# Column tiles for two matmul groups, an accumulating DMA for a bias and written slot tables in a selective-scan transformer layer

## The chip, the cores and the metric

The kernel runs on one NeuronCore of a Trainium2 chip. The metric is the time of one execution in device microseconds; less is better. A profile of one execution is beside it. Everything is float32.

## The reference, cut to what matters

Input x is 4 batches of 4096 positions with 512 channels. Per batch, six modulation rows come from a small matrix product. Then:

```
h   = layernorm(x) * (1 + ca) + sa
xs, z = split(h @ w_in.T + b_in);  z = silu(z)
dt  = softplus(xs @ w_dt.T + b_dt)
B   = xs @ w_B.T + b_B;  C = xs @ w_C.T + b_C          # 16 states each
state[n] = exp(A[n] * dt) * state[n] + dt * xs * B[n]  # along the positions
y   = (sum_n state[n] * C[n] + D * xs) * z
x   = x + ga * (layernorm(y @ w_out.T + b_out + h) * gamma + beta)
h   = layernorm(x) * (1 + cb) + sb
s   = h @ Win + bin                                    # 64 features m
g_m = sum_16(relu(s_m * W1_m + b1_m) * W2_m) + b2_m
x   = x + gb * (g @ Wout + bout)
```

The last three lines and the products for B and C are what the change rewrites on TensorE.

## The kernel before, in words

The 16384 positions are cut into 32 chunks of T = 512. The program is one software pipeline of steps `s = -1 ... 33`; step s does the scan of chunk s, the front (first norm, xs, dt, B/C, first factor u) of chunk f = s+1, the gate product, output projection and second norm of chunk b = s-1 and the feed-forward of chunk c = s-2. Every full step has U = 64 **slots**, one for each (state n, channel block j) pair of the scan, i = 4n + j.

The work of a slot goes round four engines. ScalarE (ACT) makes `exp(A dt)` into a ring of 6 (line 842, `decays`, 4 slots ahead) and `v = u * B[n]` (line 852, `input_of`). TensorE (PE) turns four 128x128 blocks of v into one of the two halves of the PSUM tile `b_ps` (`turn_v`, line 530): in slot i it makes unit i+1, and first waits for scan i-1. VectorE (DVE) runs the scan over 512 positions into a ring `hs` of 6 (`scan`, line 1140), and every second slot keeps two end states (line 1148). GpSimd (POOL) multiplies two units at a time with the row C[n], spread over the partitions by a DMA into `c_bc` (`product`, line 379; ring `pr` of 10), and for four of the 16 states folds two products with an accumulating DMA (`add_products`, line 390). TensorE transposes the products into `y_ps` and sums them there (`add_unit`, line 543), four slots after the unit, or seven for folded ones.

Beside that circuit each engine does its **side work**, written as generators: a function yields the slot from which its next part may be issued, and `Beside.until(i)` issues all parts that are due in slot i, in program order. So a slot number fixes only the place in an engine's in-order queue; the waits are on semaphores. For TensorE the side work (`dense`, line 720) is the list ORDER (lines 35 to 53): `g` (feed-forward inner sum, `add_g`, line 552, 8 matmuls), `yz` (turn y), `res` (residual, line 593), `pre` (output projection, line 600, 16), `out` (feed-forward output, `add_out`, line 579, 4), `xt` and `x2` (turn the normed rows), `z` (line 692, 16), `xs` (line 629, 16), `dt` (line 658, 16), `cb` (product for C and B, `add_cb`, line 666, 4), `bt` (turn B, line 673), `ut` (turn u) and `s` (line 716, 4). Each part has a length of 1, short ones 0.5 or 0.6; `slot(part)` and `made(part)` spread them evenly over the 64 slots in proportion to those lengths. ScalarE, VectorE, GpSimd and SP (which issues the plain DMAs) take their slots from `made` of the part that they follow, plus a small written distance. So `ut.0` is issued in slot 54, `cb.0` to `cb.3` in 48, 49, 49 and 50, `out.0` to `out.3` in 9, 11, 13 and 15, `g.0` to `g.7` in 0, 0, 1, 1, 2, 3, 3 and 5.

All side results pass through two PSUM banks `dense0` and `dense1`: `long(s, group)` is the bank of the running group, `inside(s, group)` the other one for what is done meanwhile. `tmp`, `xn`, `proj` and `x1` are shared in the same way.

The operations that the change touches are these. The C/B product is `[32 outputs] x [512 positions]` for each of four channel blocks; ScalarE adds the bias into `cb_t` [32, 512] (line 970), four small transposes turn it (line 673), SP stores the C rows (line 333). The inner sum of the feed-forward packs the 16 hidden units as 8 pairs: line 874 makes `relu` for 64 features x 2 hidden units on 128 partitions, and `w2_dg[:, k, 0:64]` (two stacked diagonals, the other 64 columns zero) sums them to 64 rows of a bank. Line 890 copies that to `gm` [128, 512] with a bias that is 1 in row 64, and line 579 multiplies a 128-position block of `gm` with `wout_g`, whose row 64 is gate times `bout`: so the output bias comes with the matmul. Line 1185 adds the bank to `x1`.

Four lines say where TensorE meets the scan:

```
pe.wait_ge(S["scan_done"], at("scan_done", s, i - 1))
for tb in range(TB):
    last = turn(b_ps[:, i % 2, tb * P:(tb + 1) * P], v[:, n % V_RING, tb, j * P:(j + 1) * P])
last.then_inc(S["b_made"], 1)
```

Of the kernel before, what the change touches and what calls it, by code (L numbers as in the profile page):

```python
def build_program(nc, ap, B, L, D, N, M, INNER):
# [8 lines left out]
    P = 128  # L10
# [24 lines left out]
    ORDER = """g.0 g.1 g.2 g.3 g.4 g.5 g.6 yz.0 g.7  # L35
        res.0 yz.1 pre.0.0 yz.2 pre.0.1 yz.3 pre.0.2 out.0 pre.0.3
        res.1 pre.1.0 out.1 pre.1.1 pre.1.2 out.2 pre.1.3
        res.2 pre.2.0 out.3 pre.2.1 pre.2.2 pre.2.3
        res.3 xt.0 pre.3.0 pre.3.1 pre.3.2 pre.3.3
        z.0.0 xt.1 z.0.1 z.0.2 xt.2 z.0.3  # L40
        xs.0.0 xt.3 xs.0.1 xs.0.2 xs.0.3
        xs.1.0 xs.1.1 xs.1.2 xs.1.3
        xs.2.0 xs.2.1 xs.2.2 xs.2.3
        xs.3.0 xs.3.1 x2.0 xs.3.2 xs.3.3
        dt.0.0 dt.0.1 x2.1 dt.0.2 dt.0.3
        dt.1.0 dt.1.1 x2.2 dt.1.2 dt.1.3
        dt.2.0 dt.2.1 x2.3 dt.2.2 dt.2.3
        dt.3.0 dt.3.1 dt.3.2 dt.3.3
        cb.0 cb.1 cb.2 cb.3
        z.1.0 z.1.1 bt.0 z.1.2 z.1.3  # L50
        z.2.0 ut.0 z.2.1 z.2.2 ut.1 z.2.3
        s.0 ut.2 s.1 s.2 ut.3 s.3
        z.3.0 z.3.1 z.3.2 z.3.3""".split()
    LENGTH = dict(yz=0.6, xt=0.6, x2=0.6, ut=0.6, bt=0.5, res=0.5)
    GROUPS = ("g", "pre.0", "pre.1", "pre.2", "pre.3", "z.0", "xs.0", "xs.1", "xs.2", "xs.3", "dt.0", "dt.1", "dt.2",
              "dt.3", "cb", "z.1", "z.2", "s", "z.3")
    BEGIN, END = {}, {}
    TOTAL = 0
    for part in ORDER:
        BEGIN[part] = TOTAL  # L60
        TOTAL += LENGTH.get(part.split(".")[0], 1)
        END[part] = TOTAL
    TOTAL += 0.8

# [17 lines left out]
    def slot(*part):  # L82
        return int(BEGIN[".".join(str(n) for n in part)] * U / TOTAL)

    def made(*part):
        return int(END[".".join(str(n) for n in part)] * U / TOTAL)


    SECOND = [made("pre", tb, 3) + (5 if tb == TB - 1 else 9 - tb) for tb in range(TB)]

    ctx = ExitStack()
    with ctx:
# [6 lines left out]
        par_d = nc.dram_tensor("par_d", (3, B, D), f32).ap()  # L99
# [7 lines left out]
        w2_dg = sb("w2_dg", [P, J, P])  # L107
# [7 lines left out]
        b_cb = sb("b_cb_col", [2 * N, 1])  # L115
# [21 lines left out]
        cb_t = sb("cb_t", [2 * N, T])  # L137
# [26 lines left out]
        gamma_r, beta_r, gain_r, shift_r = (dt_t[0:B, 1, n, :] for n in range(4))  # L164
        y_ps = pb("y_ps", [P, TB, D])
# [7 lines left out]
        def inside(s, *group):  # L173
# [3 lines left out]
        N_LATE = 6 + 5 * 2 + 2  # L177
        once = """wx_loaded wd_loaded late_loaded b2_loaded const_zeroed const_masks neg_done scal_done w2top_done
        w2dg_done b_out_loaded bout_done moved_ps moved c_exp c_one c_rcp silu_c rows_ps rows_taken mods_ps mods_done sign_done gate_done par_made
        par_stored gs_loaded wg_loaded wout_done""".split()  # L180
# [3 lines left out]
            "SP": dict(stored_0=Q, stored_1=Q, stored_2=Q, stored_3=Q, c_stored=Q),  # L184
# [46 lines left out]
        def _(sp):  # L231
# [25 lines left out]
            sp.wait_ge(S["const_zeroed"], 5)  # L257
# [3 lines left out]
            load("wd_loaded", b_cb[:, :], column("b_cb"))  # L261
# [14 lines left out]
            load("late_loaded", wout_b[0:M, :], ap["Wout"])  # L276
            load("late_loaded", wout_b[M:M + 1, :], row("bout"))
            sp.wait_ge(S["const_masks"], 2)
            load("b2_loaded", b2[0:M, :], column("b2"))
# [30 lines left out]
            STORE = [made("out", tb) + 1 for tb in range(TB)]  # L310

            def step(s, has_s, has_f, has_b, has_c):
                f, b, c = s + 1, s - 1, s - 2
                for i in range(U):
# [6 lines left out]
                    for tb in range(TB):  # L321
# [4 lines left out]
                        if has_b and i == STORE[tb] + 3:  # L326
# [3 lines left out]
                    if has_f and i == made("cb", 3) + 2:  # L330
                        sp.wait_ge(S["cb_done"], at("cb_done", f, 1))
                        sp.wait_ge(S["prod_done"], at("prod_done", f - 2, U // 2))
                        sp.dma_start(c_d[f % 2], cb_t[0:N, :]).then_inc(S["c_stored"], Q)
# [15 lines left out]
        def _(gp):  # L349
            count_up(gp, "Pool")  # L350
            for t, val in ((ident[:, :], 0.0), (w_cb[:, :, :], 0.0), (w2_dg[:, :, :], 0.0), (b2[:, :], 0.0),
                           (wout_b[:, :], 0.0)):
                gp.memset(t, val).then_inc(S["const_zeroed"], 1)
            gp.wait_ge(S["const_zeroed"], 5)

            def select(view, base, pattern):
                gp.affine_select(out=view, in_=view, compare_op=ALU.not_equal, fill=1.0, base=base, pattern=pattern,
                                 channel_multiplier=1).then_inc(S["const_masks"], 1)

            select(ident[:, :], 0, [[-1, P]])  # L360
            select(b2[:, :], -M, [[0, 1]])

# [30 lines left out]
            def attended(b):  # L393
                for tb in range(TB):
                    yield made("out", tb) + 6
                    if tb == 0:
# [4 lines left out]
                    yield made("pre", tb, 3) + 3  # L401
# [3 lines left out]
                                     ).then_inc(S["x1_done"], 1)  # L405

# [6 lines left out]
            def step_size(f, b):  # L413
                for m in range(KD):
                    yield made("dt", m, 3) + 3
# [3 lines left out]
                    yield made("dt", m, 3) + 4  # L419
# [43 lines left out]
        def _(pe):  # L463
# [83 lines left out]
            def add_g(s, c, k):  # L547
                if k == 0:
# [3 lines left out]
                mm(long(s, "g")[:, :], w2_dg[:, k, :], tmp[:, k % RELU_RING, :], start=(k == 0), stop=(k == J - 1)  # L552
                   ).then_inc(S["g_used"], 1)
# [14 lines left out]
            def add_out(s, b, c, tb):  # L568
# [10 lines left out]
                mm(to[:, :], gm[:, tb * P:(tb + 1) * P], wout_g[:, :], start=True, stop=True).then_inc(S["out_ps"], 1)  # L579
# [248 lines left out]
        def _(act):  # L828
# [503 lines left out]
```

## Time and profile before

| | |
|---|---|
| median of 3 runs | 4576.27 us (4574.64 to 4577.39) |
| the profiled execution, its own time | 4574.68 us |
| its span in the trace | 4572.9 us |
| granted TensorE clock, mean | 0.99 of full speed |
| TensorE matmul busy | 4356.8 us, 95% |
| TensorE weight load | 2784.8 us, 61% (beside the matmuls) |
| ScalarE | 3814.2 us, 83% |
| VectorE | 3698.9 us, 81% |
| GpSimd | 3596.2 us, 79% |

Busy shares alone don't say what limits: matmuls are pipelined, so the record of each is longer than the room that it takes in the stream. What one takes is read from the distance between starts. A float32 matmul call is two MATMUL records with two LDWEIGHTS; a 128x128 transpose is one record.

### The profile page before, as it was taken

The page shows a single profiled execution, that of the slowest core. Times are in us where ns is not written, and L with a number is a line of the kernel's source. Part 1 is how long each engine was busy: PE and PEld are TensorE (multiplying, and loading weights), DVE is VectorE, ACT ScalarE, POOL GpSimd, SP SyncE. Part 2 cuts the span into 40 slices and gives each one's busy share as a digit, 9 for nine tenths or more (in the row PEclk, how much of TensorE's full clock was granted, in tenths as well). Part 3 has the DMA queues.
Part 4 walks back from the last instruction along what each step waited for, and adds up shares of the span by engine and source line. Part 5 has one row for each costly group of instructions (what it writes and reads, how often), then busy time and mean ns, then how long its engine had stood idle before and what let it go on. Part 6 is the DMA issues. An engine that isn't in the chain of part 4 may idle for free. (4 is left out here: it accounts for less than half of the span.)

```text
span 4572.9 us, 69933 instructions
## 1 busy us (share of the span) xinstructions
PE 4356.8 (95%) x22528; PEld 2784.8 (61%) x22528; DVE 3698.9 (81%) x5132; ACT 3814.2 (83%) x6371; POOL 3596.2 (79%) x1999
## 2 busy tenths in 40 slices
PE   7999999999999999999999999999999999999997
PEld 3666666666666666666666666666666666666664
DVE  3778888888888888888888888888888888888885
ACT  3788888888888888888888888888888888888885
POOL 3787878887878877877878878878788878788784
PEclk8999999999999999999999999999999999999999
DMA  4233233333233333332333333332333333333322
GB/s 138 73 79 87 81 89 82 85 81 88 80 94 81 83 88 87 85 87 77 86 93 83 89 82 84 83 90 78 91 76 89 87 86 86 86 77 89 86 77 58
DMA packets 177763, 388.89 MB, mean 85 GB/s; under 512 B 22693, under 2 KB 22693, under 8 KB 177402
## 3 DMA queue, kind: packets, MB, share of 16 engines
q1 hardware_dynamic: 140538, 250.19, 17.4%
q0 software_dynamic: 36864, 134.23, 15.3%
q8 instruction: 184, 3.01, 0.3%
q14 instruction: 177, 1.45, 0.1%
HBM read 215.50 MB, written 34.63 MB: 55 GB/s over the span
## 5 line engine op out<-in xcount | busy, mean ns | idle before, releaser
L379 POOL TENSOR_TENSOR work<-work,c_bc 128x1024 f32<-128x1024 f32 x1024 | 2463.3, 2418 | 765.9 <-DVE work L1140 676.7
L1140 DVE TENSOR_TENSOR_SCAN work<-work,state,b_ps 128x512 f32<-128x512 f32 x1792 | 2257.7, 1274 | 301.1 <-PE b_ps L468 272.7
L852 ACT ACTIVATE work<-u_td,b_td 128x512 f32<-128x512 f32 x2048 | 1453.2, 710 | 163.7 <-PE b_ps L468 158.3
L842 ACT ACTIVATE work<-dt_t,neg_a 128x512 f32<-128x512 f32 x2048 | 1451.3, 709 | 4.7 <-DVE work L1140 4.4
L468 PE MATMUL b_ps<-ident,work 128*128 128x128 f32 x8192 | 1253.3, 276 | 65.0 <-DVE work L1140 57.1
L468 PEld LDWEIGHTS b_ps<-ident,work 128*128 128x128 f32 x8192 | 974.8, 142 | 505.3 <-issue 303.2
L543 PEld LDWEIGHTS y_ps<-ident,work 128*128 128x128 f32 x6144 | 740.0, 142 | 481.7 <-issue 466.0
L543 PE MATMUL y_ps<-ident,work 128*128 128x128 f32 x6144 | 862.8, 273 | 1.6 <-DMA work<-work 1.3
L692 PE MATMUL dense<-h_t,w_in_t 128*128 128x512 f32 x1024 | 514.5, 599 | 1.1 <-DVE u_td L1223 1.1
L600 PE MATMUL dense<-w_out_t,proj 128*128 128x512 f32 x1024 | 509.9, 595 | 0.0
L658 PE MATMUL dense<-xs_t,w_dt_t 128*128 128x512 f32 x1024 | 501.2, 593 | 0.0
L629 PE MATMUL dense<-h_t,w_in_t 128*128 128x512 f32 x1024 | 498.4, 595 | 1.0 <-ACT h_t L856 1.0
L1140 DVE TENSOR_TENSOR_SCAN work<-work,b_ps 128x512 f32<-128x512 f32 x256 | 307.4, 1213 | 61.5 <-PE b_ps L468 57.5
L468 PE MATMUL dense<-ident,xn 128*128 128x128 f32 x1536 | 243.6, 283 | 92.4 <-POOL xn L425 45.8
L468 PEld LDWEIGHTS dense<-ident,xn 128*128 128x128 f32 x1536 | 180.3, 144 | 226.9 <-issue 98.7
L390 POOL DMA_DIRECT2D work<-work x256 | 225.2, 880 | 81.9 <-POOL work L379 74.4
L552 PE MATMUL dense<-tmp,w_dg 128*128 128x512 f32 x512 | 245.3, 593 | 1.8 <-ACT tmp L874 1.8
L874 ACT ACTIVATE tmp<-gm,b,w 128x512 f32<-128x512 f32 x256 | 202.7, 804 | 49.4 <-PE dense L552 25.8
L692 PEld LDWEIGHTS dense<-h_t,w_in_t 128*128 128x128 f32 x1024 | 166.7, 190 | 104.1 <-issue 101.5
L629 PEld LDWEIGHTS dense<-h_t,w_in_t 128*128 128x128 f32 x1024 | 168.5, 191 | 82.9 <-issue 82.9
L417 POOL TENSOR_TENSOR dt_t<-dt_t,tmp 128x512 f32<-128x512 f32 x128 | 173.0, 1352 | 49.9 <-ACT tmp L984 49.9
L658 PEld LDWEIGHTS dense<-xs_t,w_dt_t 128*128 128x128 f32 x1024 | 165.5, 191 | 66.9 <-issue 66.9
(115 smaller groups left out, 4530.4 us busy)
## 6 DMA issues: line engine op xcount, KB each, us to landing
c_bc<-c_d SPq DMA_DIRECT2D x512, 256.0 KB, 3.3
work<-work POOLq DMA_DIRECT2D x256, 512.0 KB, 5.6
xn<-in_x SPq DMA_DIRECT2D x128, 256.0 KB, 5.1
x<-in_x SPq DMA_DIRECT2D x128, 256.0 KB, 4.3
out_dram<-x SPq DMA_DIRECT2D x128, 256.0 KB, 4.4
work<-in_wmod SPq DMA_DIRECT2D x2, 1024.0 KB, 6.5
w_in_t<-in_w_in_t SPq DMA_DIRECT2D x2, 1024.0 KB, 9.9
gain_shift<-par_d SPq DMA_DIRECT2D x8, 256.0 KB, 6.0
```

The lines of the kernel that those rows point to most:

```text
L379: gp.tensor_tensor(made_here, both(hs, HS_RING, s * U + i), c_bc[:, (s * N + n) % C_RING:(s * N + n) % C_RING + 1, :].to_broadcast([P, 2, ...
L390: gp.dma_start(both(pr, PR_RING, s * U + i), both(pr, PR_RING, s * U + i - KD), accum_op=ALU.add).then_inc(sum_done[i % KD // 2], Q)
L468: return nc.tensor.transpose(dst, src, ident[:, :])
L543: last = mm(y_ps[:, tb, j * P:(j + 1) * P], pr[:, (s * U + i) % PR_RING, tb * P:(tb + 1) * P], ident[:, :], is_transpose=True, start=(i == ...
L552: mm(long(s, "g")[:, :], w2_dg[:, k, :], tmp[:, k % RELU_RING, :], start=(k == 0), stop=(k == J - 1)).then_inc(S["g_used"], 1)
L600: last = mm(long(s, "pre", tb)[:, :], yz_t[:, k, tb * P:(tb + 1) * P], w_out[:, k, :], start=False, stop=(k == KD - 1))
L629: last = mm(long(s, "xs", m)[:, :], w_in[:, k, m * P:(m + 1) * P], h_t[:, f % 2, k, :], start=(k == 0), stop=(k == KD - 1))
L658: last = mm(long(s, "dt", m)[:, :], w_dt[:, k, m * P:(m + 1) * P], xs_t[:, k, :], start=(k == 0), stop=(k == KD - 1))
L692: last = mm(long(s, "z", m)[:, :], w_in[:, k, D + m * P:D + (m + 1) * P], h_t[:, s % 2, k, :], start=(k == 0), stop=(k == KD - 1))
L842: A(decay[:, (s * U + i) % DEC_RING, :], dt_t[:, s % 2, j, :], ACT.Exp, scale=neg_a[:, j, n:n + 1]).then_inc(S["dec_done"], 1)
L852: A(v[:, n % V_RING, tb, :], u_td[:, tb, :], ACT.Copy, scale=b_td[:, s % 2, tb, n:n + 1]).then_inc(S["v_done"], 1)
L1140: V.tensor_tensor_scan(hs[:, (s * U + i) % HS_RING, :], decay[:, (s * U + i) % DEC_RING, :], b_ps[:, i % 2, :], state[:, i:i + 1] if s % N ...
```

## The change

1. `add_cb`: each of the four matmuls of 512 positions becomes four of 128 positions, and each of these goes to its own 32 columns of the array (`tile_position=(0, tb * 32)`), so that the four blocks of positions lie on four groups of 32 partitions of the bank. The copy is [128, 128] instead of [32, 512], the turn is one 128x128 transpose instead of four 32x32, the store to DRAM is four DMAs instead of one.
2. `add_g`: each matmul of 512 positions becomes two of 256, in columns 0 to 63 and 64 to 127. The copy to `gm` has 256 elements per partition instead of 512. `add_out` then contracts 64 rows instead of 128, with `tile_position=(h * 64, 0)`.
3. The bias `bout` leaves that matmul. Once per step GpSimd issues a DMA that adds the row gate times bout to all of `x1` (`add_bout`); VectorE waits for it before line 1185. The row is made once and stored in `par_d[3]`.
4. ORDER, LENGTH, `made` and SECOND go; every part of every engine gets a written slot. The order of TensorE's parts stays as it was.
5. A few memsets and a wait at the start go.

```
    PE_AT = {}
+    for entry in """g.0@0 g.1@0 g.2@2 g.3@3 g.4@3 g.5@3 g.6@4 yz.0@4 g.7@4 res.0@6 yz.1@6 pre.0.0@6 yz.2@6 pre.0.1@6
+        yz.3@6 pre.0.2@6 out.0@6 pre.0.3@7 res.1@8 pre.1.0@8 out.1@8 pre.1.1@9 pre.1.2@9 out.2@11 pre.1.3@13
+        res.2@13 pre.2.0@14 out.3@14 pre.2.1@15 pre.2.2@15 pre.2.3@15 res.3@17 xt.0@17 pre.3.0@18 pre.3.1@18
+        pre.3.2@20 pre.3.3@20 z.0.0@21 xt.1@22 z.0.1@22 z.0.2@23 xt.2@25 z.0.3@25 xs.0.0@26 xt.3@26 xs.0.1@26
+        xs.0.2@27 xs.0.3@28 xs.1.0@28 xs.1.1@29 xs.1.2@30 xs.1.3@30 xs.2.0@32 xs.2.1@32 xs.2.2@32 xs.2.3@33
+        xs.3.0@33 xs.3.1@34 x2.0@34 xs.3.2@34 xs.3.3@34 dt.0.0@34 dt.0.1@34 x2.1@38 dt.0.2@38 dt.0.3@40
+        dt.1.0@40 dt.1.1@40 x2.2@40 dt.1.2@40 dt.1.3@41 dt.2.0@41 dt.2.1@42 x2.3@42 dt.2.2@42 dt.2.3@42
+        dt.3.0@44 dt.3.1@48 dt.3.2@48 dt.3.3@48 cb.0@51 cb.1@51 cb.2@51 cb.3@51 z.1.0@52 z.1.1@52 bt.0@52
+        z.1.2@52 z.1.3@53 z.2.0@56 ut.0@56 z.2.1@56 z.2.2@56 ut.1@56 z.2.3@58 s.0@59 ut.2@59 s.1@59 s.2@59
+        ut.3@60 s.3@61 z.3.0@61 z.3.1@61 z.3.2@62 z.3.3@62""".split():
+        part, first = entry.split("@")
+        PE_AT[part] = int(first)
+    AT = dict(
+        store=(0, 10, 10, 13),
+        load=(7, 11, 17, 17),
+        c_store=50,
+        xsh=(15, 17, 18, 22),
+        x1=(16, 17, 26, 26),
+        bout=36,
+        dt_add=(41, 43, 49, 52),
+        u_mul=(41, 44, 52, 52),
+        gate=(26, 57, 57, 6),
+        relu=(62, 63, 0, 2, 2, 2, 2, 3),
+        gm=3,
+        skip=(9, 10, 10, 11),
+        rstdx=14,
+        xn=(15, 15, 16, 16),
+        t2=(12, 17, 18, 26),
+        rstd2=30,
+        xn2=(30, 30, 30, 30),
+        h2=(32, 39, 41, 42),
+        h=(18, 24, 25, 27),
+        xs=(30, 30, 31, 36),
+        cb=50,
+        bt=54,
+        edt=(41, 43, 43, 52),
+        ldt=(41, 43, 47, 52),
+        ez=(28, 59, 59, 0),
+        lz=(28, 59, 59, 0),
+        sig=(28, 59, 59, 5),
+        y_copy=(2, 3, 3, 3),
+        yz=(5, 6, 7, 7),
+        out=(7, 10, 12, 15),
+        pre=(8, 13, 16, 21),
+        dt=(40, 41, 43, 51),
+        ut=(56, 57, 59, 60),
+        z=(26, 55, 58, 63),
+        s=62,
+        stx=(1, 9, 12, 13),
+        nmrx=14,
+        st2=(18, 21, 27, 31),
+        nmr2=31,
+    )
...
+            def add_bout(b):
+                yield AT["bout"]
+                gp.wait_ge(S["par_stored"], 4 * Q)
+                gp.wait_ge(S["xn2_done"], at("xn2_done", b, TB))
+                gp.dma_start(x1[:, :, :], par_d[3:4, b // NC:b // NC + 1, :].to_broadcast([P, TB, D]),
+                             accum_op=ALU.add).then_inc(S["bout_added"], Q)
...
             # add_g
-                mm(long(s, "g")[:, :], w2_dg[:, k, :], tmp[:, k % RELU_RING, :], start=(k == 0), stop=(k == J - 1)
-                   ).then_inc(S["g_used"], 1)
+                for h in range(2):
+                    last = mm(long(s, "g")[h * M:(h + 1) * M, 0:T // 2], w2_dg[:, k, :],
+                              tmp[:, k % RELU_RING, h * (T // 2):(h + 1) * (T // 2)], start=(k == 0), stop=(k == J - 1),
+                              tile_position=(0, h * M))
+                last.then_inc(S["g_used"], 1)
...
             # add_out
-                mm(to[:, :], gm[:, tb * P:(tb + 1) * P], wout_g[:, :], start=True, stop=True).then_inc(S["out_ps"], 1)
+                h = tb // 2
+                mm(to[:, :], gm[h * M:(h + 1) * M, tb % 2 * P:(tb % 2 + 1) * P], wout_g[h * M:(h + 1) * M, :], start=True,
+                   stop=True, tile_position=(h * M, 0)).then_inc(S["out_ps"], 1)
...
             # add_cb, turn_b
-                last = mm(long(s, "cb")[0:2 * N, :], w_cb[:, k, :], xs_t[:, k, :], start=(k == 0), stop=(k == KD - 1))
+                for tb in range(TB):
+                    last = mm(long(s, "cb")[tb * 2 * N:(tb + 1) * 2 * N, 0:P], w_cb[:, k, :],
+                              xs_t[:, k, tb * P:(tb + 1) * P], start=(k == 0), stop=(k == KD - 1),
+                              tile_position=(0, tb * 2 * N))
...
-                for tb in range(TB):
-                    last = nc.tensor.transpose(inside(s, "z.1")[:, tb * 2 * N:(tb + 1) * 2 * N],
-                                               cb_t[:, tb * P:(tb + 1) * P], ident[0:2 * N, 0:2 * N])
-                last.then_inc(S["bt_ps"], 1)
+                turn(inside(s, "z.1")[:, 0:P], cb_t[:, :]).then_inc(S["bt_ps"], 1)
...
             # take_out (VectorE)
+                    dve.wait_ge(S["bout_added"], (c + 1) * Q)
```

## Rows read from the trace of the kernel before

**Rows 1.** The page: span, busy time by engine, and the granted clock in 40 slices

```profile
span 4572.9 us, 69933 instructions
...
PE 4356.8 (95%) x22528; PEld 2784.8 (61%) x22528; DVE 3698.9 (81%) x5132; ACT 3814.2 (83%) x6371; POOL 3596.2 (79%) x1999
...
PEclk8999999999999999999999999999999999999999
```

**Rows 2.** Line 1164, the copy of s, once per step: first and last start

```profile
L1164 DVE COPY gm<-dense x32: 690/691/692, 352.6 to 4555.1; 128x512 f32<-128x512 f32 x32
```

**Rows 3.** Timeline of TensorE around C/B: start us, us, what, count [idle before]

```profile
2125.82 1.88 PE L658 MATMUL dense<-xs_t,w_dt_t 128*128 128x512 f32 x4
2127.54 0.60 PE L543 MATMUL y_ps<-ident,work 128*128 128x128 f32 x4
2127.98 0.60 PE L468 MATMUL b_ps<-ident,work 128*128 128x128 f32 x4
2128.51 1.04 PE L666 MATMUL dense<-xs_t,w_cb_t 128*32 128x512 f32 x2
2129.48 0.66 PE L468 MATMUL b_ps<-ident,work 128*128 128x128 f32 x4
2130.07 1.90 PE L666 MATMUL dense<-xs_t,w_cb_t 128*32 128x512 f32 x4
2131.90 0.66 PE L468 MATMUL b_ps<-ident,work 128*128 128x128 f32 x4
...
2134.43 0.60 PE L468 MATMUL b_ps<-ident,work 128*128 128x128 f32 x4
2134.86 1.02 PE L692 MATMUL dense<-h_t,w_in_t 128*128 128x512 f32 x2
2135.72 0.60 PE L468 MATMUL b_ps<-ident,work 128*128 128x128 f32 x4
2136.26 0.43 PE L673 MATMUL dense<-ident,cb_t 32*128 32x32 f32 x4
2136.62 1.12 PE L692 MATMUL dense<-h_t,w_in_t 128*128 128x512 f32 x2
```

**Rows 4.** Groups by line: shapes xcount | busy us, mean ns | idle before <-releaser

```profile
L379 POOL TENSOR_TENSOR work<-work,c_bc 128x1024 f32<-128x1024 f32 x1024 | 2463.3, 2418 | 765.9 <-DVE work L1140 676.7 <-issue 87.6 <-PE y_ps L543 0.5
L1140 DVE TENSOR_TENSOR_SCAN work<-work,state,b_ps 128x512 f32<-128x512 f32 x1792 | 2257.7, 1274 | 301.1 <-PE b_ps L468 272.7 <-POOL work L379 24.2 <-ACT work L842 0.8
...
L468 PE MATMUL b_ps<-ident,work 128*128 128x128 f32 x8192 | 1253.3, 276 | 65.0 <-DVE work L1140 57.1 <-ACT work L852 7.2
...
L1148 DVE TENSOR_REDUCE state<-work 128x2 f32<-128x2 f32 x1024 | 132.9, 130 | 0.0
...
L1238 DVE TENSOR_SCALAR tmp<-dense,b_z_col 128x512 f32<-128x512 f32 x128 | 94.9, 741 | 0.0
L1233 DVE TENSOR_SCALAR sz_t<-dense,b_z_col 128x512 f32<-128x512 f32 x128 | 94.5, 739 | 57.8 <-PE dense L692 56.6 <-issue 1.1
```

**Rows 5.** Who waited for whom: us in total, times, longest us

```profile
PE b_ps L468 <- DVE work L1140: 57.1, 80, 4.2
...
PE dense L468 <- POOL xn L425: 45.8, 32, 2.8
...
PE dense L468 <- ACT xn L912: 18.7, 31, 1.2
...
PE dense L468 <- ACT xs_t L964: 14.1, 30, 0.7
```

**Rows 6.** Line 390, the accumulating DMAs: their issue on GpSimd, and their landing

```profile
L390 POOL DMA_DIRECT2D work<-work x256: 878/878/1216, 90.4 to 4482.5; - x128
...
DMA to landing us min/median/max: 4.5/5.6/8.1
```

**Rows 7.** The chain that ended last, in order of time: start us, us, what

```profile
4556.88 7.12 PE dense L552 x16
...
4564.07 0.70 ACT gm L890
```

More of the change, by code:

```diff
@@ L30, in build_program @@
     SKIP_AT = (8, 10)
[L35 to L53, printed above, removed]
@@ L54, in build_program @@
-    LENGTH = dict(yz=0.6, xt=0.6, x2=0.6, ut=0.6, bt=0.5, res=0.5)
     GROUPS = ("g", "pre.0", "pre.1", "pre.2", "pre.3", "z.0", "xs.0", "xs.1", "xs.2", "xs.3", "dt.0", "dt.1", "dt.2",
               "dt.3", "cb", "z.1", "z.2", "s", "z.3")
[L57 to L63, printed above, removed]
+    PE_AT = {}
+    for entry in """g.0@0 g.1@0 g.2@2 g.3@3 g.4@3 g.5@3 g.6@4 yz.0@4 g.7@4 res.0@6 yz.1@6 pre.0.0@6 yz.2@6 pre.0.1@6
[10 more added lines that the diff above has]
+        PE_AT[part] = int(first)
@@ L82, in slot @@
     def slot(*part):
[L83 to L89, printed above, removed]
+        return PE_AT[".".join(str(n) for n in part)]
     ctx = ExitStack()
@@ L136, in build_program @@
         u_td = sb("u_td", [P, TB, D])
-        cb_t = sb("cb_t", [2 * N, T])
+        cb_t = sb("cb_t", [P, P])
         b_td = sb("b_td", [P, 2, TB, N])
@@ L164, in build_program @@
         gamma_r, beta_r, gain_r, shift_r = (dt_t[0:B, 1, n, :] for n in range(4))
+        bout_r, bias_r = (x1[0:B, n, :] for n in range(2))
         y_ps = pb("y_ps", [P, TB, D])
@@ L260, in _ @@
             load("wd_loaded", b_dt[:, :], ap["b_dt_c"])
-            load("wd_loaded", b_cb[:, :], column("b_cb"))
+            for tb in range(TB):
+                load("wd_loaded", b_cb[tb * 2 * N:(tb + 1) * 2 * N, :], column("b_cb"))
             load("wd_loaded", neg_a[:, :, :], ap["A_log_c"])
@@ L275, in _ @@
                     load("late_loaded", dst[h * M:(h + 1) * M, :], ap[src][:, h * J:(h + 1) * J])
[L276 to L279, printed above, removed]
+            for h in range(2):
+                load("late_loaded", wout_b[h * M:(h + 1) * M, :], ap["Wout"])
+                load("b2_loaded", b2[h * M:(h + 1) * M, :], column("b2"))
             def store_gates():
@@ L283, in store_gates @@
                 sp.dma_start(par_d[2], gate_b).then_inc(S["par_stored"], Q)
+                load("bout_row", bout_r, row("bout").to_broadcast([B, D]))
                 sp.wait_ge(S["par_made"], 2)
@@ L308, in spread_c @@
                              ).then_inc(c_loaded[(k * N + n) % C_RING], Q)
-            STORE = [made("out", tb) + 1 for tb in range(TB)]
+            STORE = AT["store"]
             def step(s, has_s, has_f, has_b, has_c):
@@ L325, in step @@
                                          ).then_inc(S[f"stored_{tb}"], Q)
-                        if has_b and i == STORE[tb] + 3:
+                        if has_b and i == AT["load"][tb]:
                             sp.wait_ge(S[f"stored_{tb}"], at(f"stored_{tb}", c, Q))
@@ L329, in step @@
                                          ).then_inc(xb_loaded[tb], Q)
-                    if has_f and i == made("cb", 3) + 2:
+                    if has_f and i == AT["c_store"]:
                         sp.wait_ge(S["cb_done"], at("cb_done", f, 1))
                         sp.wait_ge(S["prod_done"], at("prod_done", f - 2, U // 2))
-                        sp.dma_start(c_d[f % 2], cb_t[0:N, :]).then_inc(S["c_stored"], Q)
+                        for tb in range(TB):
+                            sp.dma_start(c_d[f % 2][:, tb * P:(tb + 1) * P], cb_t[tb * 2 * N:tb * 2 * N + N, :]
+                                         ).then_inc(S["c_stored"], Q)
                     if s == 0 and i == 17:
@@ L350, in _ @@
             count_up(gp, "Pool")
[L351 to L361, printed above, removed]
+            gp.memset(ident[:, :], 0.0).then_inc(S["const_zeroed"], 1)
+            gp.wait_ge(S["const_zeroed"], 1)
+            gp.affine_select(out=ident[:, :], in_=ident[:, :], compare_op=ALU.not_equal, fill=1.0, base=0,
+                             pattern=[[-1, P]], channel_multiplier=1).then_inc(S["const_masks"], 1)
             def both(ring, of, i):
@@ L400, in attended @@
                                      ).then_inc(S["xsh_done"], 1)
-                    yield made("pre", tb, 3) + 3
+            def attended(b):
+                for tb in range(TB):
+                    yield AT["x1"][tb]
                     gp.wait_ge(S["xsh_done"], at("xsh_done", b, tb + 1))
@@ L418, in step_size, with inputs @@
                                      ).then_inc(S["dt_done"], 1)
-                    yield made("dt", m, 3) + 4
+            def inputs(f, b):
+                for m in range(KD):
+                    yield AT["u_mul"][m]
                     if m == 0:
@@ L969, in front @@
                 act.wait_ge(S["bt_ps"], at("bt_ps", f, 0))
-                A(cb_t[:, :], long(s, "cb")[0:2 * N, :], ACT.Identity, bias=b_cb[:, :]).then_inc(S["cb_done"], 1)
-                yield made("bt", 0)
+                A(cb_t[:, :], long(s, "cb")[:, 0:P], ACT.Identity, bias=b_cb[:, :]).then_inc(S["cb_done"], 1)
+                yield AT["bt"]
                 act.wait_ge(S["bt_ps"], at("bt_ps", f, 1))
@@ L998, in sigmoids @@
                 for m in range(KD - 1):
-                    yield from sigmoid(s, m, made("z", m, 3) + 1)
+                    yield from sigmoid(s, m)
             AHEAD = DEC_RING - 2
```

119 lines of the change are left out of this document (63 added, 56 removed).

## The prediction

> **What bounds the kernel now.** I read the page first: TensorE is busy 95% of the span at the full of its two clock levels (nines in every slice but the first, so 2.4 GHz), the three others 79 to 83% [rows 1]. A full step takes (4555.1 - 352.6) / 31 = 135.56 us [rows 2], 2.12 us per slot.
>
> Busy time says too much of TensorE, so I went to its timeline and took distances between starts [rows 3]. Four MATMUL records of line 658 (two calls) are followed 1.72 us later by the next group: **0.86 us per call of 512 columns**, 0.43 per record. Four transposes take **0.44**. With 84 such calls and 132 groups of four transposes a step needs 84 x 0.86 + 132 x 0.44 = 130.3 us, and about 1.1 more for what is special around C/B (next part). So 4 of 135.56 us are idle: TensorE's stream sets the step. GpSimd's product waits for the scan for 677 us in all, 21 us per step [rows 4]; it has room, and ScalarE and VectorE are idle for 17% and 19% of the span.
>
> The view of waits tells where TensorE's idle time comes from: for the scan 57.1 us, for u from GpSimd (line 425) 45.8, for the normed rows 18.7, for xs 14.1 [rows 5].
>
> **The change, part by part** (per step, times 32).
>
> *Edges of a tile.* The timeline shows a price that no group shows. Four turns before a C/B call take 0.53 instead of 0.44 (2127.98 to 2128.51), and two records of line 666 take 0.97 instead of 0.86 (2128.51 to 2129.48) [rows 3]. So going from the full array to a smaller tile and back costs about **0.11 us per edge**; the weight load can't run ahead there. C/B had three runs, six edges. The four 32-row turns cost 0.36 us plus 0.10 for their entry.
>
> *C/B.* Before: 4 x 0.86 + 6 x 0.11 = 4.10. After: all parts stand in slot 51, one run, two edges. The run has 32 records of 128 columns, each a quarter of 0.43, 0.107. Within one tile two records must follow each other; I take it that the second record of a tile runs beside the first of the next tile, so that 32 records take the room of 17: 17 x 0.107 + 0.22 = 2.04. Saves 2.06. The turn goes from 0.46 to 0.11: saves 0.35.
>
> *Inner sum.* Before: 8 x 0.86 = 6.88, no edges. After: 32 records of 256 columns (0.213 each); the slots (0, 0; 2; 3, 3, 3; 4, then yz.0; 4) make five runs, ten edges. With the same overlap a run of n calls has the room of 2n+1 records: (16 + 5) x 0.213 + 10 x 0.11 = 5.57. Saves 1.31.
>
> *Feed-forward output.* Contracting 64 rows instead of 128 streams the same 512 columns; four separate runs add eight edges: costs 0.88. No row shows a 64-row tile; the nearest is the 32-row tile of line 673 with 0.10 at its entry. Bounds: nothing, and the whole 0.36 of that group per run, 1.4.
>
> Stream: -2.06 - 0.35 - 1.31 + 0.88 = **-2.84 us, -91 us in all**. No row shows two tiles at once, so overlap is the unknown. Without any: C/B 32 x 0.107 + 0.22 = 3.64 (-0.46), turn -0.35, inner sum 32 x 0.213 + 1.1 = 7.92 (+1.04), output +0.88: +1.11, **+36 us**. I take overlap between neighbours only. The Trainium skill (TensorEngine Tiling (Array Packing), Key Properties) says that changing the tiling mode drains TensorE: the 0.11 us per edge of rows 3 agrees. The same section says that different tiles load and multiply in parallel, and its table gives up to 4x for 32 columns: by that C/B would take 4 x 0.86 / 4 + 0.22 = 1.1 us, another 30 us less in all.
>
> *Copies.* `cb_t` and `gm` get shorter on ScalarE, which has room: nothing in the steps. In the tail they and the inner sum are on the chain: 7.12 us for 16 records become 17 x 0.213 = 3.6, and the copy of 0.70 loses some 0.3 [rows 7]. **-4 us.**
>
> *The accumulating DMA.* On GpSimd it costs an issue of 0.88 us, or up to four times that since it names four times as many rows [rows 6]: 3.5 us, against 21 us of room. VectorE's new wait for it stands 35 slots (75 us) later, with the next scans queued behind it, and lands at once. Who could be hurt is the queue's next user: the folded product of units 36 and 37, needed by TensorE in slot 43. Product 2.4 us [rows 4], landing 5.6 [rows 6], from scan 37 on: ready near slot 42. The bias DMA has twice the bytes just ahead of it; if they are served in turn it comes up to 5.6 us late, and TensorE would wait up to about 3 us per step. All landings in rows 6 lie between 4.5 and 8.1 us, and two slots of margin (4 us) cover half of the spread that the bias can add, so I take nothing and keep +3 us x 32 = +96 as the far end.
>
> *The written slots: SP, GpSimd, ScalarE.* SP stops from slot 0 until VectorE's `out.0` (slot 7) and has the C row of slot 12 behind it: 4 slots, 8.5 us, more than any landing of rows 6. The C store is four issues instead of one, 6 slots before use. GpSimd's gates 1 and 2 (slot 57) wait for ScalarE's slot 59 and VectorE's slot 58: the products behind them come some 5 us later, out of 21. ScalarE waits at 50 for TensorE's 51 and at 3 for its 4, with four decays ahead already. Nothing for all of these; the cover is the rings of six (`hs`, decay), and once it is used up each us is one of the scan's.
>
> *The written slots: TensorE.* `ut.0` goes from slot 54 to 56 while u is still finished in GpSimd's slot 52: the 45.8 us of waiting goes. The normed rows and xs[2] are taken one or two slots earlier on ScalarE: half of 18.7 + 14.1, 16. **-62 us.** Against that the work is lumped. TensorE can make unit i+1 only after scan i-1, so where it has little side work it waits for VectorE. A scan is 1.27 us, the states 0.13 every second slot, a `z` 1.48 [rows 4]. Slots 35 to 37: TensorE 3 x 0.88 = 2.6, VectorE 3.9. Slots 49 and 50: 0.88 against 2.7. Slots 53 to 55: 2.6 against 5.4. That is 5.9 us; the even table had some 0.5 of it (53 to 55: 5.6 against 6.1). With no lead at all it gives 5.4 us per step back, 173 us. But `b_ps` has two halves and before each of these stretches stands a lump (slots 34, 48, 52: 3.0 to 5.2 us) in which VectorE draws level, so I let one scan of 1.27 per stretch be covered: 0 + 0.5 + 1.5 - 0.5 = 1.5, **+48 us**.
>
> Sum: 4574.7 - 91 - 4 - 62 + 48 = 4465.7, **4466 us**. The profiled execution is 1.6 us below the median of the runs, less than the sum can tell, so it stands for the median too.
>
> **The rivals.**
> 1. *The tiles don't overlap.* Each record then takes its own columns in turn; sum +36 instead of -91: 4574.7 + 36 - 1 - 62 + 48 = 4596. For it: in rows 3 a 32-column call takes 0.86 like a full one and no row has two tiles at work; float32 calls come as two records of the same tile. Against it: every record brings its own weights, and rows show these loads hidden behind the matmul before.
> 2. *The lumps cost more than the columns give: slower.* TensorE waits for the scan in slots 35 to 37, 49, 50, 53 to 55, uncovered, and by the same count in 16 to 19 (6.1 against 7.8 us: 1.7 more). That is 7.1 us per step, 227 us: 4574.7 - 91 - 4 - 62 + 227 = 4645. It decides from 157 us, 4.9 us per step; at three quarters of it the time would be 4588. For it: the sum over slots of the longer of both engines grows from 150 to 160 us. Against it: the same sum said 150 before and the step took 135.6, so most of such unevenness is covered.
> 3. *The table closes nearly all waits.* No give-back, and the waits of rows 5 except the one for the scan go (78.6): 4574.7 - 91 - 4 - 79 = 4401, and less with full overlap of four tiles (4371).
> 4. *The change doesn't do what it says.* The counts would show it: 32 records each for lines of `g` and `cb`; only if the tile position were ignored would it be rival 1.
>
> **How the numbers follow.** Forecast (neighbours overlap, lumps mostly covered): 0.52, own range 4420 to 4520. Rival 1: 0.19 (4575 to 4615). Rival 2: 0.15 (4570 to 4660), which also stands for the late folded sum. Rival 3: 0.14 (4365 to 4420). The range 4385 to 4605 leaves out the lower part of rival 3 and the upper part of 1 and 2. A measurement of this kernel can tell about 0.2%, 9 us, from no change. Faster: 0.52 + 0.14 + 0.04 from rivals 1 and 2 = 0.70; same 0.09; slower 0.21.
>
> **What would show it.** In the timeline after: 32 records of the C/B line in about 2 us, and starts of two tiles in one matmul's room; two calls of the inner sum in about 1.1 us. In the waits: u from GpSimd gone, the scan's wait before `b_ps` near 100 us, not 230. A folded product that TensorE waits for would show as a wait of line 543 for a DMA. The step by the copy of s would be near 132.2 us. Wrong it is if the C/B run takes 3.6 us, or if TensorE's stream falls and the step doesn't.

## The result and the profile after

The changed kernel takes **4469.16 us** (median of 4, 4467.86 to 4469.99) against 4575.45 us (4 runs, 4574.47 to 4577.39): ratio 0.9767, 95% interval 0.9750 to 0.9784. The forecast was 4466 us, and the range holds the result. The agreement of the total is better than that of its terms.

The page of the kernel after: span, busy times, granted clock.

```profile
span 4466.1 us, 72589 instructions
...
PE 4267.7 (96%) x23712; PEld 2729.8 (61%) x23712; DVE 3680.3 (82%) x5133; ACT 3816.1 (85%) x6371; POOL 3629.6 (81%) x2026
...
PEclk8999999999999999999999999999999999999998
```

TensorE is busy for 89 us less (4356.8 before [rows 1]), and the granted clock looks the same in the slices. The copy of s gives the step: (4449.6 - 346.2) / 31 = 132.37 us against 135.56 [rows 2].

```profile
L1206 DVE COPY gm<-dense x32: 677/681/692, 346.2 to 4449.6; 128x512 f32<-128x512 f32 x32
```

The timeline of TensorE around C/B, to be read against [rows 3]:

```profile
2078.99 1.04 PE L501 MATMUL b_ps<-ident,work 128*128 128x128 f32 x8
2081.16 0.63 PE L501 MATMUL b_ps<-ident,work 128*128 128x128 f32 x4 [1.13 <-DVE work L1182]
2081.72 1.08 PE L705 MATMUL dense<-xs_t,w_cb_t 128*32 128x128 f32 x32
2082.73 0.66 PE L501 MATMUL b_ps<-ident,work 128*128 128x128 f32 x4
2083.73 1.98 PE L730 MATMUL dense<-h_t,w_in_t 128*128 128x512 f32 x4 [0.35 <-DVE tmp L1258]
```

32 records fill 2081.72 to 2082.73, and 0.11 of that is the edge: **0.90 us**, the room of four tiles at once (4 x 0.86 / 4), not the 1.82 of neighbours in pairs. One line above, the second wait that my sum spoke of: two groups of turns (0.87 us of room) and 1.3 us of nothing before the next. These are slots 49 and 50.

The inner sum, and one run of the output matmul:

```profile
2110.81 0.60 PE L501 MATMUL b_ps<-ident,work 128*128 128x128 f32 x4
2111.34 1.08 PE L586 MATMUL dense<-tmp,w_dg 128*64 128x256 f32 x8
2112.36 0.66 PE L501 MATMUL b_ps<-ident,work 128*128 128x128 f32 x4
...
2114.16 0.60 PE L501 MATMUL b_ps<-ident,work 128*128 128x128 f32 x4
2114.70 0.65 PE L586 MATMUL dense<-tmp,w_dg 128*64 128x256 f32 x4
2115.38 0.63 PE L501 MATMUL b_ps<-ident,work 128*128 128x128 f32 x4
2116.07 2.06 PE L586 MATMUL dense<-tmp,w_dg 128*64 128x256 f32 x12
2118.07 0.66 PE L501 MATMUL b_ps<-ident,work 128*128 128x128 f32 x4
```

```profile
2000.11 1.04 PE L501 MATMUL b_ps<-ident,work 128*128 128x128 f32 x8
2001.08 1.12 PE L616 MATMUL dense<-wout_g,gm 64*128 64x512 f32 x2
2002.13 0.66 PE L576 MATMUL y_ps<-ident,work 128*128 128x128 f32 x4
```

Two calls with their edge take 1.02 us (2 x 0.43 + 0.11 and a little more), as fully overlapped tiles should. But three calls take 2.00 where 1.40 would do: their relus come one every 0.71 us (four in 2.91 us at 2115.22). A single output call takes 1.05 instead of 0.86, its entry 0.10 more: about 0.29 for its two edges, 1.2 us per step, where I had 0.88.

Groups by line after (busy us, mean ns | idle before and who ended it), the new DMA with its landing, and the end of the chain that ended last:

```profile
L501 PE MATMUL dense<-ident,xn 128*128 128x128 f32 x1536 | 239.7, 280 | 22.8 <-ACT xn L977 8.7 <-POOL xn L458 6.1 <-ACT xn L950 2.1
...
L463 POOL TENSOR_TENSOR sz_t<-sz_t,tmp 128x512 f32<-128x512 f32 x128 | 172.3, 1346 | 177.7 <-ACT tmp L1035 177.7
...
L586 PEld LDWEIGHTS dense<-tmp,w_dg 128*64 128x64 f32 x1024 | 53.6, 135 | 80.3 <-ACT tmp L912 57.4 <-issue 18.2
L434 POOL DMA_DIRECT2D x<-par_d x32 | 51.7, 1615 | 5.2 <-ACT xn L977 5.2
```

```profile
L434 POOL DMA_DIRECT2D x<-par_d x32: 1319/1625/1652, 293.0 to 4439.5; - x32
...
DMA to landing us min/median/max: 9.5/10.2/10.7
```

```profile
4451.12 5.04 ACT tmp L912 x7
...
4456.21 0.68 PE dense L586 x4
...
4456.96 0.48 ACT gm L928
```

TensorE's idle time before the turns of u and of the normed rows is 22.8 us instead of 92.4. Weight loads of the inner sum wait 57 us for a relu (9 before), and GpSimd's gates wait 178 us for ScalarE (9 before). In the tail the inner sum's seven relus (5.04 us, 0.72 each) are now the chain and TensorE only ends it: relus and sum took 7.1 us before [rows 7] and take 5.8 now.

Two waits of the turns of v, for the scan and for ScalarE's v (57.1 [rows 5] and 7.2 us before [rows 4]):

```profile
PE b_ps L501 <- DVE work L1182: 66.5, 91, 3.9
...
PE b_ps L501 <- ACT work L890: 18.4, 33, 3.4
```

### The profile page after: what moved, and what is told of

It is laid out like the page before. It is cut to its first block and busy times, and to the rows that moved or that the text cites. A ratio compares the mean times of both kernels' runs of the same rounds, so it can differ in the third digit from the quotient of the medians.

```text
span 4466.1 us, 72589 instructions
## 1 busy us (share of the span) xinstructions
PE 4267.7 (96%) x23712; PEld 2729.8 (61%) x23712; DVE 3680.3 (82%) x5133; ACT 3816.1 (85%) x6371; POOL 3629.6 (81%) x2026
## 5 line engine op out<-in xcount | busy, mean ns | idle before, releaser
L501 PE MATMUL b_ps<-ident,work 128*128 128x128 f32 x8192 | 1246.7, 278 | 93.0 <-DVE work L1182 66.5
L501 PEld LDWEIGHTS b_ps<-ident,work 128*128 128x128 f32 x8192 | 945.7, 142 | 499.3 <-issue 266.1
L576 PEld LDWEIGHTS y_ps<-ident,work 128*128 128x128 f32 x6144 | 724.7, 142 | 299.0 <-issue 294.6
L730 PE MATMUL dense<-h_t,w_in_t 128*128 128x512 f32 x1024 | 505.1, 597 | 10.7 <-DVE tmp L1258 10.7
L638 PE MATMUL dense<-w_out_t,proj 128*128 128x512 f32 x1024 | 498.0, 594 | 0.0
L667 PE MATMUL dense<-h_t,w_in_t 128*128 128x512 f32 x1024 | 493.1, 595 | 1.0 <-ACT h_t L894 1.0
L463 POOL TENSOR_TENSOR sz_t<-sz_t,tmp 128x512 f32<-128x512 f32 x128 | 172.3, 1346 | 177.7 <-ACT tmp L1035 177.7
L501 PE MATMUL dense<-ident,xn 128*128 128x128 f32 x1536 | 239.7, 280 | 22.8 <-ACT xn L977 8.7
L447 POOL TENSOR_TENSOR dt_t<-dt_t,tmp 128x512 f32<-128x512 f32 x128 | 182.8, 1428 | 51.4 <-ACT tmp L1024 51.4
## 6 DMA issues: line engine op xcount, KB each, us to landing
x<-par_d POOLq DMA_DIRECT2D x32, 1024.0 KB, 10.2
```

The lines of the kernel that those rows point to most:

```text
L501: return nc.tensor.transpose(dst, src, ident[:, :])
L576: last = mm(y_ps[:, tb, j * P:(j + 1) * P], pr[:, (s * U + i) % PR_RING, tb * P:(tb + 1) * P], ident[:, :], is_transpose=True, start=(i == ...
L638: last = mm(long(s, "pre", tb)[:, :], yz_t[:, k, tb * P:(tb + 1) * P], w_out[:, k, :], start=False, stop=(k == KD - 1))
L667: last = mm(long(s, "xs", m)[:, :], w_in[:, k, m * P:(m + 1) * P], h_t[:, f % 2, k, :], start=(k == 0), stop=(k == KD - 1))
L730: last = mm(long(s, "z", m)[:, :], w_in[:, k, D + m * P:D + (m + 1) * P], h_t[:, s % 2, k, :], start=(k == 0), stop=(k == KD - 1))
```

## The experiments

All are timed beside the kernel before; the 95% interval of each ratio is 0.0010 to 0.0017 to either side. In the code, AT and PE_AT are the tables of the diff.

**Tables and tiles apart.** `tiles_old_table` is the change with all slots of the kernel before:

```diff
-PE_AT, AT: the written slots
+PE_AT, AT: the values that ORDER, made and SECOND gave (ut.0@54, cb 48 49 49 50, ...)
```

> The change with its tiles, its bias DMA and its edges, but with every part in the slots of the kernel before. The theory from the trace after (four tiles overlap fully, so that the stream loses 4.6 us per step, and the written slots cost 1.4 us per step): 4575 - 147 - 4 = 4424 us, that is faster than the change. The prediction's own reading (neighbours overlap, -2.84 us per step, and the written slots bring 0.4): 4575 - 91 - 4 = 4480 us, slower than the change.

4618.39 us, ratio 1.0094 (1.0079 to 1.0109): neither. With the old slots the tiles make the kernel **slower by 43 us**. The timeline of TensorE in it, and the windows (us, busy, clock, DMA) over the same stretch:

```profile
2016.19 0.60 PE L452 MATMUL b_ps<-ident,work 128*128 128x128 f32 x4
2020.55 0.66 PE L452 MATMUL dense<-ident,xn 128*128 128x128 f32 x4 [3.76 <-POOL xn L409]
2021.04 0.60 PE L452 MATMUL b_ps<-ident,work 128*128 128x128 f32 x4
2021.48 3.53 PE L681 MATMUL dense<-h_t,w_in_t 128*128 128x512 f32 x4
2024.81 0.69 PE L527 MATMUL y_ps<-ident,work 128*128 128x128 f32 x4
```

```profile
2018.50:2020.50 2.00, 0.00 (x0) 1.00 1.07 217
2020.50:2022.50 2.00, 1.95 (x10) 0.77 0.59 113
2022.50:2024.50 2.00, 2.00 (x3) 0.50 0.00 0
2024.50:2026.50 2.00, 2.00 (x14) 0.88 0.10 12
```

C/B and its turn take some 2.4 us less of the stream, u is no sooner: TensorE waits 3.76 us for GpSimd's last product of u, and the next four records of z take 3.33 us instead of 1.72. The granted clock falls to 0.50 there, the lower of the two levels (1.2 GHz), about 1 us behind the idle stretch (0.77 over the 2 us from 2020.50). All 31 steps with this wait show it: the clock over these four records is 0.50 to 0.69. The wait is 119 us in all instead of 45.8, 2.3 us more per step, and the slow records cost 1.6: 3.9 us per step, 125 us, more than the 94 that the tiles bring without it (next run). The Trainium skill (TensorE: Matmul & The Clock Gate, HAM oscillation — how this bites in real kernels) warns of just this, a wait that sends the array to half clock each time round; the trace agrees. How long an idle stretch must be, these runs don't say; its length alone doesn't decide it (`relus_early` below).

`table_only` is the kernel before with the written slots, no tiles and no bias DMA.

> The kernel before, with the slots of the change written in and no tiles, no bias DMA. If the written slots cost 1.4 us per step: 4575 + 45 = 4620 us. By the prediction (-62 for waits, +48 for lumps): 4561 us. If the table was the main gain: under 4500 us.

4563.13 us, ratio 0.9971 (0.9961 to 0.9981): 12.5 us faster; my terms for the slots, -62 and +48, made -14. The group of turns by line in it, and the run of C/B in its timeline:

```profile
L495 PE MATMUL dense<-ident,xn 128*128 128x128 f32 x1536 | 238.7, 280 | 21.2 <-ACT xn L966 8.7 <-POOL xn L452 4.6 <-ACT xn L939 2.1
```

```profile
2127.41 3.62 PE L693 MATMUL dense<-xs_t,w_cb_t 128*32 128x512 f32 x8
2130.97 0.66 PE L495 MATMUL b_ps<-ident,work 128*128 128x128 f32 x4
```

That is 71 us less idle time than the 92.4 of the same group before. C/B stands in one run of 3.56 us here, with two edges instead of six: 0.44 us per step, another 14 us that the slots bring and that I had booked to the tiles. So of 85 us, 12.5 arrive and some 73 come back elsewhere. One place is a wait that I had put at nothing: the turns wait 32.7 us for ScalarE's v, 7.2 before. So with the written slots the tiles bring 4563.1 - 4469.2 = 94 us, without them they cost 43: the two parts of the change don't add.

`tiles_old_ut_later` tests the cause: the old slots and the tiles, with one part moved. `z.2.1` and `z.2.2` (slot 55) stand behind `ut.0` in TensorE's order, so they come in slot 56 too.

```diff
-ut.0@54   AT ut=(55, 56, 58, 60)
+ut.0@56   AT ut=(56, 57, 59, 60)
```

> The tiles with the slots of before (4618 us), but the first turn of u in slot 56 instead of 54 and its copies one slot later. If tiles lose under the old slots because TensorE, done with C/B sooner, then waits up to 3.8 us for u and runs the next z at half clock: the 119 us of waiting for u and 32 x 1.65 = 53 us of slow records go, 4618 - 172 = 4446 us, with some given back 4450 to 4490. If the old slots are bad as a whole (many small waits), under 50 us of it come back: over 4570 us.

4529.74 us, ratio 0.9897: 89 of the 172 us are back, halfway between the two theories. The wait for u (16.1 us in all now) is the largest single loss and one slot number decides it; what is left shows as 1.7 us per step between two groups of turns at the same place, where `z.2.1` and `z.2.2` stood and the turns now wait for ScalarE's v, and as many small waits. The kernel before with `ut.0` in slot 56 alone was not run, so how much of the 89 us the move would bring without tiles is open.

**How tiles overlap.** `cb_tile_by_tile` runs the 16 calls of C/B with the tile as the outer loop.

```diff
-for k: for tb: mm(tile tb, block k)
+for tb: for k: mm(tile tb, block k)
```

> The change, with the 32 records of C/B ordered tile by tile (all four channel blocks of one tile, then the next tile) instead of channel block by channel block. If tiles overlap because consecutive calls lie in different tiles, the run goes from 0.9 us to 32 x 0.107 = 3.4 us, TensorE gets 2.5 us per step more: up to 4469 + 80 = 4549 us. If the overlap doesn't depend on the order (each call is short for another reason), the run stays at 0.9 us and the time at 4469.

4500.66 us, ratio 0.9837, 31 us slower than the change. Its timeline:

```profile
2097.08 2.46 PE L707 MATMUL dense<-xs_t,w_cb_t 128*32 128x128 f32 x32
2099.47 0.66 PE L501 MATMUL b_ps<-ident,work 128*128 128x128 f32 x4
```

The same 32 records take 2.3 us instead of 0.90. So overlap hangs on the order: neighbouring calls must lie in different tiles. But it isn't 3.4 us either: the starts in the trace pair the last four records of a tile with the first four of the next, so at most two tiles run at once. The 1.4 us more in the run cost 0.98 us per step: two thirds come through.

`cb_plain` is the change with C/B in its old form, under the written slots.

> The change, with only C/B in its old form (four calls of 512 columns in one tile, four small turns, one store). Its run would take 4 x 0.86 = 3.4 us instead of 0.9, and the turn 0.35 more: 2.9 us per step, 4469 + 92 = 4561 us if all of it lies on the path, so that C/B alone would carry the whole gain of the tiles and the feed-forward's tiles nothing. By the prediction's stream terms C/B carries 2.4 us (77 us, 4546) and the feed-forward 0.4 us. If the room refills other waits, as tile by tile did (2.3 us against 0.9 for 31 us): 4525.

4549.72 us, ratio 0.9943. **C/B brings 80.6 us of the change, the feed-forward's tiles 13.4** (4563.1 - 4549.7, together with the bias DMA and the edits of the start). My stream terms were 77 and 14. The run is 2.5 us shorter than in one tile and the turn 0.35, 92 us, and most of it arrives.

**The bias DMA.** `no_bias_dma` leaves out the accumulating DMA and its wait, and so the output bias of the feed-forward.

> The change without the accumulating DMA of the output bias and the wait for it; the bias of the feed-forward is left out of the result. By the prediction nothing hangs on it: 4469 within 9 us. The rival (its 1.6 us of issue and 1 MB ahead of the folded products cost TensorE or the scan something): faster by 20 to 96 us.

4466.35 us against 4469.16: 3 us, nothing. Its issue is 1.6 us, within my bounds; it lands after 10.2 us, later than any DMA of rows 6, but TensorE waits for a folded product only 1.9 us in all.

**GpSimd's gates.** `gates_later` issues the gates behind the sigmoids that they wait for.

```diff
-AT gate=(26, 57, 57, 6)
+AT gate=(29, 60, 61, 6)
```

> The change, with GpSimd's gates 0 to 2 issued in slots 29, 60 and 61 instead of 26, 57 and 57, behind the sigmoids that they wait for. GpSimd's 178 us of waiting there go. If the scan's 116 us of waiting for GpSimd lie on the path: faster by 20 to 60 us, 4410 to 4450. If TensorE's stream sets the step and these waits lie beside it: 4469 within 9 us.

4509.78 us, ratio 0.9856: slower by 41 us, which no theory had. VectorE's busy time rose from 3680 to 3723 us, and one group carries all of it. Timelines of VectorE and of GpSimd in the same stretch:

```profile
2062.19 2.31 DVE L1155 SCALAR_TENSOR_TENSOR norm<-norm 128x4 f32<-128x4 f32 x1 [0.74 <-ACT norm L931]
2064.42 1.27 DVE L1142 TENSOR_TENSOR_SCAN work<-work,state,b_ps 128x512 f32<-128x512 f32 x1
```

```profile
2060.60 1.57 POOL L423 TENSOR_TENSOR sz_t<-sz_t,tmp 128x512 f32<-128x512 f32 x1
2061.84 2.62 POOL L359 TENSOR_TENSOR work<-work,c_bc 128x1024 f32<-128x1024 f32 x1
```

An operation on four elements per partition takes 2.31 us. It starts at 2062.19, and it ends (2064.50) when GpSimd's product does (2061.84 + 2.62 = 2064.46). In the change it takes 1.0 us and ends with a product too. In the kernel before the same operation takes 0.16 us where no product runs:

```profile
2197.91 0.16 DVE L1153 SCALAR_TENSOR_TENSOR norm<-norm 128x4 f32<-128x4 f32 x1
```

The trace of the change has 1.0 us in nearly every step and that of `gates_later` 2.3; 32 x 1.3 are the 41 us. `gates_12_later` leaves gate 0 at 26:

> gates_later lost 40 us. In its trace the small norm operation of VectorE with two SBUF inputs (128x4, second norm, slot 31) takes 2.3 us instead of 1.0: it ends with GpSimd's product. If that is the cause, the harm came from gate 0 alone (slot 26 to 29 shifts the products under slot 31): with gate 0 back at 26 and gates 1 and 2 at 60 and 61 the norm operation takes 1.0 us again and the time is 4469 within 9 us. If the late gates 1 and 2 did the harm: near 4510.

4468.13 us, the change's time. The group in `gates_later` and in `gates_12_later`:

```profile
L1155 DVE SCALAR_TENSOR_TENSOR norm<-norm 128x4 f32<-128x4 f32 x64 | 85.0, 1328 | 24.3 <-ACT norm L931 23.7 <-ACT norm L905 0.6
```

```profile
L1155 DVE SCALAR_TENSOR_TENSOR norm<-norm 128x4 f32<-128x4 f32 x64 | 42.8, 669 | 24.3 <-ACT norm L931 23.7 <-ACT norm L905 0.6
```

GpSimd waits in its gates for 89 us in `gates_12_later` (gate 0) instead of 178. So the 88 us of waiting in gates 1 and 2 cost nothing, and moving gate 0 by three slots costs 41 us through the place where a product then lies. `nmr_by_scalar` takes the collision away:

```diff
-V.scalar_tensor_tensor(norm[:, n, :, 8:9], norm[:, n, :, 6:7], -1.0, norm[:, n, :, 9:10], mult, mult)
+for tb: V.tensor_scalar(norm[:, n, tb, 8:9], norm[:, n, tb, 6:7], norm[:, n, tb, 9:10], -1.0, mult, mult)
```

> The change, with that norm operation (mean times minus one times rstd, two SBUF tensors in) done as four operations with one tensor and one per-partition scalar each. If a two-tensor operation of VectorE waits for GpSimd's running product and these don't: four take 0.3 to 0.5 us instead of 1.0 and the four xn2 start earlier: faster by 10 to 25 us, near 4450. If the small operation was slow for itself, or its wait is hidden: 4469 within 9 us.

4456.60 us, ratio 0.9741: **12.6 us faster than the change** with four operations in place of one. The group, and one place in the timelines of VectorE and of GpSimd:

```profile
L1196 DVE TENSOR_SCALAR norm<-norm 128x1 f32<-128x1 f32 x256 | 36.6, 206 | 24.3 <-ACT norm L971 23.7 <-ACT norm L945 0.6
...
691.14 0.58 DVE L1196 TENSOR_SCALAR norm<-norm 128x1 f32<-128x1 f32 x4 [0.74 <-ACT norm L971]
...
689.76 2.36 POOL L399 TENSOR_TENSOR work<-work,c_bc 128x1024 f32<-128x1024 f32 x1
```

The four are done in 0.58 us while the product runs on for 0.40 us: 0.4 us per step less than 1.0, 13 us in all. Two tensors from SBUF wait for GpSimd's product, one tensor and a scalar don't. The Trainium skill (SBUF — State Buffer, Summary: rules for kernel authors) says that when VectorE has two SBUF inputs and GpSimd's operation reads SBUF, the second of them to issue is blocked until the first is done; these runs agree. `nmr_by_scalar` with gate 0 moved later was not run, so what gate 0's own wait of 89 us costs is open.

**The lumps.** `fill_49_50` fills the empty slots.

```diff
-cb.0..3@51  z.1.0@52 z.1.1@52   dt=(40,41,43,51) edt=(..,52) ldt=(..,52) dt_add=(..,52) u_mul=(41,44,52,52) bt=54
+cb.0..3@49  z.1.0@51 z.1.1@51   dt=(40,41,43,50) edt=(..,51) ldt=(..,51) dt_add=(..,51) u_mul=(41,44,51,52) bt=53
```

> The change, with C/B in slot 49 instead of 51, the first two calls of z.1 in 51, and the last dt copy and what follows it one slot earlier. The trace of the change shows 1.8 us per step lost between the turns of slots 49 and 50, where TensorE has nothing but them. If that is a loss of its own: up to 32 x 1.8 = 58 us, 4411 to 4450 us. If those slots give VectorE the time that it needs anyway, the wait moves to the next turns: 4469 within 10 us.

4463.72 us, ratio 0.9752 (0.9735 to 0.9768). The 1.3 us between those turns go, but the gain is 5 us, inside the uncertainty. The wait moves: the 0.5 us before the first call of z.1 become 1.1, and the turns of u wait for GpSimd 20.9 us in all instead of 6.1. (The 1.8 us of the expectation are the 1.3 and the 0.5 together.) `fill_and_nmr` has both edits.

> Both: C/B in slot 49 (fill_49_50, 4464 us) and the norm operation by scalars. If they add up: 4464 minus what nmr_by_scalar brings, 4440 to 4455 us, faster than both kernels. If not: 4464.

**4452.17 us, ratio 0.9731 (0.9716 to 0.9745)**, the fastest kernel of the study, 17 us under the change.

**Why the feed-forward's tiles bring little.** `relus_early` builds on `fill_and_nmr`:

```diff
-AT relu=(62, 63, 0, 2, 2, 2, 2, 3)
+AT relu=(62, 63, 0, 0, 1, 1, 2, 2)
```

> fill_and_nmr (4452 us) with ScalarE's relus 3 to 7 in slots 0, 1, 1, 2, 2 instead of 2, 2, 2, 2, 3. Under the written slots the feed-forward's tiles brought only 13 us (table_only 4563 against cb_plain 4550), although its calls take half the room: in the trace three calls take 2.0 us instead of 1.4, held by relus of 0.8 us each (58 us of waiting before their weight loads). If ScalarE's slots are what holds them: 58 us of waits go and the time falls by 20 to 50 us, to 4400 to 4430. If the relus come no sooner (they wait for the ring of three) or the wait moves: 4452 within 9 us.

4498.88 us, ratio 0.9836: 47 us slower. The relus do come sooner (weight loads wait 5 us for them, not 58), but they stand ahead of ScalarE's v:

```profile
2128.42 0.65 PE L546 MATMUL dense<-tmp,w_dg 128*64 128x256 f32 x4
2131.07 1.07 PE L461 MATMUL b_ps<-ident,work 128*128 128x128 f32 x4 [2.00 <-ACT work L850]
2132.07 2.73 PE L546 MATMUL dense<-tmp,w_dg 128*64 128x256 f32 x12
2134.73 0.66 PE L461 MATMUL b_ps<-ident,work 128*128 128x128 f32 x4
```

TensorE is idle for 2.00 us until v is there, in every step (66.0 us in all instead of 5.8), and then twelve records of the inner sum take 2.66 us instead of 2.00, at half clock again (0.50 from 2132 to 2134). In 20 of 30 steps the clock fell so behind the same 2.00 us; in the other 10 it stayed high, and there the twelve records take 1.45 us. So the relus no longer hold them: 0.55 us per step, 18 us, is what the relus had cost there. ScalarE's order in slots 0 to 3 must feed both; whether the feed-forward's tiles can bring more is open.

## Why the prediction was right

**The bound and the step** were read rightly: TensorE's stream sets the step, which was to be near 132.2 us and is 132.37.

**C/B: right in size, wrong in its run.** I took it that a record overlaps only with its neighbour (1.82 us); the runs show four tiles at once, 0.90. The factor that the Trainium skill gives (TensorEngine Tiling (Array Packing), Theoretical Speedup), up to 4x for 32 columns, is reached in this run. That my 77 us came near the measured 80.6 is luck, with two causes: the merging of three runs into one (14 us), which I booked to the tiles, belongs to the slots, and about an eighth of what the stream saves (92 us) is given back in waits.

**Inner sum and output.** Measured 13.4 us together, forecast 14, again by cancellation: the calls are fully overlapped (0.43 each, better than forecast), but the 64-row runs cost 0.29 instead of 0.22, and relus that come one every 0.71 us now hold calls of 0.43. The price of an edge, 0.11 us, stood up at both column tiles.

**The slots.** -14 forecast, -12.5 measured in `table_only`, and this too is luck: the -12.5 have in them the 14 us of merging C/B's runs, which I had counted elsewhere. The waits for u, the normed rows and xs went (71 us where I had 62), and some 73 came back where I had 48. The scan's wait, which I expected near 100 us after the change, is only 66.5, so most of it came back in other waits, among them the one for ScalarE's v, which I had put at nothing. The uncovered idle between the turns of slots 49 and 50 was 0.5 us in my sum and is 1.3 us in the timeline, while filling it moves the time by 5 us only: the lump term was too small as a sum, and wrong slot by slot.

**The step that failed** is the additivity. I costed `ut.0` at 45.8 us, its wait in the kernel before, as if tiles and slots didn't meet there. They do: with the tiles that wait becomes 119 us and the clock falls behind it; under the old slots the tiles lose 43 us, and with `ut.0` moved the same kernel is 46 us under the one before. The order of adding the parts (slots first) happens to be the one in which my two terms come out near what was measured.

**The rivals.** 1 (no overlap) is refuted by the 0.90 us. 2 (uncovered lumps) and 3 (all waits closed) didn't come. Of the costs at nothing the bias DMA and gates 1 and 2 were right, and the trace shows no product of GpSimd waiting for a C row from SP; ScalarE's waits were not nothing (the turns' wait for v went from 7.2 to 18.4 us). The copy and sum in the tail, -4, was some -1.5, since the relus became the chain.

## What to carry to other kernels

A faster part gives nothing if the next consumer waits for something that didn't get faster; where the low clock level followed that idle stretch, as here behind 3.76 us, it cost twice, so a tile change and the place of the next wait belong together. Put neighbouring small matmuls into different column tiles, in runs as long as possible, since each change of tile size costs 0.11 us. Look at tiny VectorE operations that take over a microsecond: here one with two SBUF operands waited for the end of a GpSimd product, and one with a scalar operand didn't.

## What the runs showed that I had not expected

Four 32-column tiles run at once in float32, 32 records in 0.90 us; ordered tile by tile they take 2.3, not 3.4. A 3.76 us wait of TensorE was followed by records at half clock in every step, a 2.00 us wait in 20 of 30. And a shift of one GpSimd operation by three slots cost 41 us through a four-element operation on VectorE that lasted 2.31 us.
